# A four-block sequence kernel: the state-space block's norm by batch inside the first feed-forward, its fused input weights made there

## Reference

```python
x = x + _L0_attn_ref(_layernorm(x), ...)   # 16 heads, softmax with a page mask
x = x + _L0_ffn_ref(_layernorm(x), ...)    # top-2 of 8 experts, and a shared expert
x = x + _L1_attn_ref(_layernorm(x), ...)   # state-space block
x = x + _L1_ffn_ref(_layernorm(x), ...)    # top-2 of 8 experts, and a shared expert
# start of _L1_attn_ref, x already normed:
h = x @ fc1_w.T + fc1_b
xz = h @ in_proj_w.T
xc, z = jnp.split(xz, 2, axis=-1)
u = sum((xp[:, w:w + L, :] * conv_w[:, w] for w in range(d_conv))) + conv_b   # four taps, xp is xc padded
u = jax.nn.silu(u)
```

## Time and profile before

| | |
|---|---|
| median of 3 runs | 1397.61 us (1397.1 to 1402.02) |
| the profiled execution | 1397.69 us, of which the span of its instructions is 1395.9 us |
| PE busy | 1239.8 us, 89% of the span |
| DVE busy | 1092.1 us, 78% |
| ACT busy | 851.8 us, 61% |
| POOL busy | 575.7 us, 41% |
| mean granted TensorE clock | 0.932 of full speed |

### The profile page before, as it was taken

How to read it: one execution, slowest core, us unless ns; L and a number is a source line. 1 busy time by engine, 2 the same in 40 slices (tenths; PEclk the granted TensorE clock), 3 DMA queues, 4 the chain that set the end, 5 groups by cost and what they waited for, 6 DMA issues and landing times. The chain is left out here.

```text
span 1395.9 us, 23363 instructions
## 1 busy us (share of the span) xinstructions
PE 1239.8 (89%) x8438; PEld 646.3 (46%) x8438; DVE 1092.1 (78%) x1318; ACT 851.8 (61%) x1506; POOL 575.7 (41%) x428
## 2 busy tenths in 40 slices
PE   4936999999899989899996877999999999976998
PEld 2411333334343435344443334555655556564665
DVE  5768899999899556856554966999999999864554
ACT  2523899989799643232222778989999899512221
POOL 2320010000101237666575024888888888820000
PEclk9965999999999989999996986999999999975999
DMA  4331121321211155332450001222232232111231
GB/s 111 113 115 30 52 64 46 95 67 54 77 53 50 41 98 163 99 102 95 120 96 20 0 6 47 102 93 92 96 101 91 91 104 93 61 29 24 60 62 38
DMA packets 70509, 103.09 MB, mean 74 GB/s; under 512 B 12718, under 2 KB 42230, under 8 KB 70406
## 3 DMA queue, kind: packets, MB, share of 16 engines
q1 hardware_dynamic: 69110, 100.39, 24.6%
q10 hardware_dynamic: 1296, 1.33, 0.3%
HBM read 87.92 MB, written 13.37 MB: 73 GB/s over the span
## 5 line engine op out<-in xcount | busy, mean ns | idle before, releaser
L638 DVE TENSOR_REDUCE att_found<-PS 128x2 f32<-128x1024 f32 (+2 forms) x288 | 333.3, 1219 | 18.9 <-PE PS L747 17.2
L714 ACT ACTIVATE att_prob<-PS 128x512 f32<-128x512 f32 x576 | 313.5, 596 | 46.2 <-PE PS L769 34.4
L1928 POOL TENSOR_TENSOR ms_ch<-xnT,ms_c_rows 128x1024 f32<-128x1024 f32 x103 | 243.9, 2368 | 45.6 <-PE PS L1838 33.6
L1838 PE MATMUL PS<-ms_ch,ident_sb 128*128 128x512 f32 x512 | 241.4, 594 | 0.9 <-POOL ms_ch L1928 0.9
L1889 DVE TENSOR_TENSOR_SCAN xnT<-xnT,PS 128x1024 f32<-128x1024 f32 x103 | 231.1, 2268 | 7.4 <-PE PS L1829 7.1
L1867 ACT ACTIVATE ms_scaled<-m_dtu_turns,m_bt 128x256 f32<-128x256 f32 x448 | 191.6, 495 | 29.6 <-PE PS L1829 29.6
L788 PE MATMUL PS<-att_prob,att_v 128*32 128x256 f32 (+1 forms) x2560 | 184.9, 375 | 2.8 <-ACT fr_out L703 2.6
L1829 PEld LDWEIGHTS PS<-ident_sb,ms_scaled 128*128 128x128 f32 x1024 | 120.6, 144 | 80.1 <-DVE xnT L1889 37.4
L747 PE MATMUL PS<-kr,qr 55*128 55x128 bf16 (+4 forms) x1152 | 121.6, 292 | 31.2 <-PEq L260 16.0
L1829 PE MATMUL PS<-ident_sb,ms_scaled 128*128 128x128 f32 x1024 | 137.0, 278 | 9.7 <-ACT ms_scaled L1867 4.6
L769 PE MATMUL PS<-qr,kr 55*128 55x128 bf16 (+4 forms) x1152 | 115.9, 279 | 15.7 <-ACT att_prob L714 8.4
(11 more groups left out here) (225 smaller groups left out, 1739.4 us busy)
## 6 DMA issues: line engine op xcount, KB each, us to landing
ms_c_rows<-bc_rows_dram SPq DMA_DIRECT2D x64, 512.0 KB, 3.7
f_gate_row<-gate_rows_dram SPq DMA_DIRECT2D x64, 256.0 KB, 3.5
f_mask_row<-mask_rows_dram SPq DMA_DIRECT2D x64, 128.0 KB, 3.1
qk_parts_dram<-qkv_parts SPq DMA_DIRECT2D x48, 128.0 KB, 1.9
heads_dram<-fr_out SPq DMA_DIRECT2D x16, 256.0 KB, 2.6
f_mask_row<-mask_rows_dram SPq DMA_DIRECT2D x64, 64.0 KB, 3.2
qr<-qk_parts_dram SPq DMA_DIRECT2D x32, 96.0 KB
qr<-qk_parts_dram SPq DMA_DIRECT2D x96, 32.0 KB
```

Source lines behind the costliest of these rows:

```text
L638: dve.tensor_reduce(found[:, :, pair, first:first + (n - 1) * step + 1:step], PS[:, bank:bank + 2, :].rearrange("p r (w n) -> p r w n", w= ...
L714: act.activation(prob[:, step % PROB_RING * GH + h, :], PS[:, SCORE_BANK + unit % SCORE_RING, :], ACT.Exp, scale=float(D) ** -0.5).then_in ...
L1838: last = pe.matmul(PS[:, Y_BANK + 2 * half + q, :], g.ident[:, :], ch[:, half, q * CH:(q + 1) * CH], start=n == 0, stop=n == NS - 1)
L1928: pool.tensor_tensor(ch[:, half, :], decay_then_h(s, half), c_rows[:, s % C_RING, :], ALU.mult).then_inc(ch_ready, 1)
```

## The change

- The norm of the state-space block is taken out of its block. `Front`'s methods get batches 4 to 7 (batch 4 is batch 0 for the second time, and so on). In `first_ffn`, chunks 5, 6 and 7 norm batches 0, 1 and 2: in each, DVE does `moments_half` in slot e=1, `moments_rest` in e=2, `normalize` in e=5 and e=6; POOL does `root` in e=3; PE does `turn_x` in e=6 and e=7; ACT does `store_x` in e=7 and after it. Batch 3 is normed after the last chunk's statistics, still inside the block.
- The five weights that the first products of `mamba_in` need are loaded by SP at the start of `first_ffn`, ahead of the first gate rows, into a row buffer `shared_row`, which later serves as the scan's extra half row. PE makes the fused weight in chunk 4, slot 0 (2 large and 8 small matmul instructions), ACT copies it out in slot 2.
- The block `norm_transpose` visit 1 is gone, and with it one meeting of all engines. The other eight loads (`m`: d, x_proj, dt_proj, dt_b, a_log, fc2_b; `m.last`: two) are issued by SP at the start of `mamba_in`. DVE, ACT and PE wait for `m` only behind the convolutions; POOL waits for it where it did, ahead of its add of fc2_b to X.

```diff
     g.stat_steps, g.rstd_ready, g.normed, g.transposed, g.stored = (
...
     def turn_bank(self, b, k):
-        return (k, 2 + k, k, 1 - k)[b]
+        return (k, 2 + k, k, 1 - k)[b] if b < B else k
...
     def tiles(self, b):
-        return slice(TB * b, TB * (b + 1))
+        return slice(TB * (b % B), TB * (b % B + 1))
...
+        if b < B:
+            dve.wait_ge(self.stats_done, CPB * (b + 1))
+        else:
+            dve.wait_ge(stats_done, CPB * (b - B + 1))
         steps.done(dve.tensor_tensor(tmp[:, 0, :], me, mo, ALU.add))
...
-            last = dve.tensor_scalar(self.xn[:, k, j, :], self.g.X[:, TB * b + n, :], self.mean[:, n:n + 1], self.rstd[:, n:n + 1],
+            last = dve.tensor_scalar(self.xn[:, k, j, :], self.g.X[:, TB * (b % B) + n, :], self.mean[:, n:n + 1], self.rstd[:, n:n + 1],
...
+        if (b, k) == (4, 1):
+            pe.wait_ge(self.rows_stored, 8)
+        if b >= B:
+            pe.wait_ge(self.x_stored, CPB * (b - 1) + k + 1)
         for j in range(TPC):
...
         act.wait_ge(self.transposed, c + 1)
-        act.activation(self.g.xnT[:, CH * c:CH * (c + 1)], self.g.PS[:, self.turn_bank(b, k), :], ACT.Copy).then_inc(self.x_stored, 1)
+        act.activation(self.g.xnT[:, CH * (c % NCH):CH * (c % NCH + 1)], self.g.PS[:, self.turn_bank(b, k), :], ACT.Copy).then_inc(self.x_stored, 1)
...
         @block.sync
         def _(sp):
+            for dst, src in early.pairs:
+                sp.dma_start(dst, src).then_inc(early.loaded, 16)
             for c in range(NCH):
                 for e in range(NE):
...
+                    if c >= NORM_AT and e == 3:
+                        f.root(pool, B + c - NORM_AT)
+            f.root(pool, 2 * B - 1)
 
         @block.scalar
...
                             f.store_rows(act, b)
                             f.store_row_tables(act, b)
+                    if (c, e) == (4, 2):
+                        act.wait_ge(fused, 1)
+                        act.activation(early.in_proj.rearrange("p a b -> p (a b)"), PS[:, FUSED, :], ACT.Copy).then_inc(fused_stored, 1)
+                        act.activation(early.b_in_x, PS[:, FUSED_B, 0:2 * DI], ACT.Copy).then_inc(fused_stored, 1)
+                    if c >= NORM_AT and e >= NE - 1:
+                        f.store_x(act, B + c - NORM_AT, e - NE + 1)
             chunks(act, chunk)
+            for part in range(CPB):
+                f.store_x(act, 2 * B - 1, part)
+            act.wait_ge(f.x_stored, 2 * NCH)
 
         @block.vector
...
                         f.normalize(dve, 3, part)
+                if c >= NORM_AT:
+                    b = B + c - NORM_AT
+                    if e == 1:
+                        f.moments_half(dve, b, stats_ready)
+                    if e == 2:
+                        f.moments_rest(dve, b)
+                    if e in (5, 6):
+                        f.normalize(dve, b, e - 5)
...
             staggered(dve, chunk)
             finish(NCH - 1)
             stats(NCH - 1)
-            dve.wait_ge(stats_ready, NCH)
+            f.moments(dve, 2 * B - 1, stats_ready)
+            for part in range(CPB):
+                f.normalize(dve, 2 * B - 1, part)
...
                     for b, at, part in ((2, (0, 4), 0), (2, (0, 5), 1), (3, (3, 3), 0), (3, (3, 4), 1)):
                         if (c, e) == at:
                             f.logits(pe, b, part)
+                    if (c, e) == (4, 0):
+                        pe.wait_ge(early.loaded, early.all)
+                        pe.wait_ge(f.x_stored, NCH)
+                        pe.wait_ge(f.route_steps, 3 * ROUTE_STEPS + f.SCORES)
+                        pe.matmul(PS[:, FUSED, :], early.fc1, early.in_proj.rearrange("p a b -> p (a b)"), start=True, stop=True)
+                        for j in range(2 * DI):
+                            last = pe.matmul(PS[:, FUSED_B, j:j + 1], early.in_proj[:, j, :], early.fc1_b, start=True, stop=True)
+                        last.then_inc(fused, 1)
+                    if (c, e) == (4, 7):
+                        pe.wait_ge(fused_stored, 2)
                     for b, at in ((2, (2, 0)), (3, (4, 7))):
                         if (c, e) == at:
                             f.turn_rows(pe, b)
+                    if c >= NORM_AT and e >= NE - 2:
+                        f.turn_x(pe, B + c - NORM_AT, e - NE + 2)
                 up(NS - 1, sw1[:, 1, :], x)
                 second(NE - 1)
                 third(NS - 1, sw2[:, 1, :], x)
             staggered(pe, chunk)
             finish(NCH - 1, 1)
+            for part in range(CPB):
+                f.turn_x(pe, 2 * B - 1, part)
 
 
...
+
+def mamba_early(nc, ctx, g):
+
+    m = Loads(nc, ctx, "me_w")
+    row = g.shared_row
+    m.fc1, m.in_proj, m.fc1_b = row[:, 0:P], row[:, P:5 * P].rearrange("p (j c) -> p j c", c=P), row[:, 5 * P:5 * P + 1]
+    at = 5 * P + 1
+    m.conv_w, m.conv_b = row[:, at:at + DI * KC].rearrange("p (d t) -> p d t", t=KC), row[:, at + DI * KC:at + DI * (KC + 1)]
+    at += DI * (KC + 1)
+    m.b_in_x = row[:, at:at + 2 * DI]
+    for name in ("fc1", "in_proj", "fc1_b", "conv_w", "conv_b"):
+        m.to(dict(fc1=m.fc1, in_proj=m.in_proj, fc1_b=m.fc1_b, conv_w=m.conv_w, conv_b=m.conv_b)[name], g.w[name])
+    return m
 
 
...
     m.ctx = early
-    m.fc1, m.in_proj = m.tensor("fc1", [P, P], g.w["fc1"]), m.tensor("in_proj", [P, 2 * DI, P], g.w["in_proj"])
-    m.fc1_b = m.tensor("fc1_b", [P, 1], g.w["fc1_b"])
-    m.conv_w, m.conv_b = m.tensor("conv_w", [P, DI, KC], g.w["conv_w"]), m.tensor("conv_b", [P, DI], g.w["conv_b"])
     m.x_proj = m.tensor("x_proj", [P, DI, 2 * NS + R], g.w["x_proj"])
...
-        fc1, in_proj, x_proj, dt_proj = m.fc1, m.in_proj, m.x_proj, m.dt_proj
-        fc1_b, conv_w, conv_b, dt_b, a_log, fc2_b = m.fc1_b, m.conv_w, m.conv_b, m.dt_b, m.a_log, m.fc2_b
-        w_in_x, b_in_x = sb("w_in_x", [P, 2 * DI, P]), sb("b_in_x", [P, 2 * DI])
+        x_proj, dt_proj, dt_b, a_log, fc2_b = m.x_proj, m.dt_proj, m.dt_b, m.a_log, m.fc2_b
...
         @block.sync
         def _(sp):
+            for group in (m, m.last):
+                for dst, src in group.pairs:
+                    sp.dma_start(dst, src).then_inc(group.loaded, 16)
             for c in range(NCH):
...
@@ -1563,13 +1624,9 @@
         @block.scalar
         def _(act):
             act.preload_act_table(ACT.Silu)
-            act.wait_ge(m.loaded, m.all)
+            act.wait_ge(early.loaded, early.all)
             act.wait_ge(pad_set, 1)
             act.sem_inc(xc_ready, 1)
-            act.wait_ge(fused, 1)
-            act.activation(w_in_x[:, :, :].rearrange("p a b -> p (a b)"), PS[:, 6, :], ACT.Copy).then_inc(fused_stored, 1)
-            act.activation(b_in_x[:, :], PS[:, 7, 0:2 * DI], ACT.Copy).then_inc(fused_stored, 1)
-            act.wait_ge(fused_stored, 2)
 
             def take_x(b, k, c):
                 act.wait_ge(x_done, c + 1)
...
 
             act.preload_act_table_set("natural_log_exp_and_others")
+            act.wait_ge(m.loaded, m.all)
             act.activation(m.a[:, :, :], a_log[:, :, :], ACT.Exp).then_inc(a_steps, 1)
...
         @block.vector
         def _(dve):
             dve.sem_inc(conv_steps, 2 * CONV)
-            dve.wait_ge(m.loaded, m.all)
+            dve.wait_ge(early.loaded, early.all)
...
                                 dve.wait_ge(conv_steps, steps.base + steps.n - 1)
                                 steps.mark(dve.scalar_tensor_tensor(conv[:, k, half, :], x, w, conv[:, k, half, :], ALU.mult, ALU.add))
+            dve.wait_ge(m.loaded, m.all)
             dve.wait_ge(a_steps, 1)
...
         def _(pe):
             pe.sem_inc(u_ready, 2 * DI)
             pe.sem_inc(z_ready, 2)
-            pe.wait_ge(m.loaded, m.all)
-
-            pe.matmul(PS[:, 6, :], fc1[:, :], in_proj[:, :, :].rearrange("p a b -> p (a b)"), start=True, stop=True)
-            for j in range(2 * DI):
-                last = pe.matmul(PS[:, 7, j:j + 1], in_proj[:, j, :], fc1_b[:, :], start=True, stop=True)
-            last.then_inc(fused, 1)
-            pe.wait_ge(fused_stored, 2)
             with pe.Fori(0, B) as b:
...
                     last.then_inc(z_done, 1)
             pe.wait_ge(u_ready, DI * (2 + NCH))
             pe.wait_ge(z_ready, 2 + NCH)
+            pe.wait_ge(m.loaded, m.all)
 
...
-        four_halves, one_half = g.xnT[:, :].rearrange("p (r t) -> p r t", t=T), sb("one_half", [P, T])
+        four_halves, one_half = g.xnT[:, :].rearrange("p (r t) -> p r t", t=T), g.shared_row
         c_rows, ch = sb("c_rows", [P, C_RING, T]), sb("ch", [P, DI, T])
...
         g = make_globals(nc, ctx, w, out)
+        early = mamba_early(nc, ctx, g)
         with ExitStack() as scope:
...
-            with ExitStack() as early:
-                m = mamba_loads(nc, scope, early, g)
-                norm_transpose(nc, g, 1, [m, m.last])
-                mamba_in(nc, g, m)
+            with ExitStack() as inner:
+                m = mamba_loads(nc, scope, inner, g)
```

(3 more changed lines are left out.)

25 lines of the change are left out of this document (14 added, 11 removed).

## The result

The changed kernel takes 1422.28 us in the median of 4 runs (1417.12 to 1426.54), the kernel before 1397.36 beside it (4 runs, 1393.58 to 1402.02). The ratio is 1.0163, with a 95% interval from 1.0131 to 1.0195: 22.8 us slower by the ratio (24.9 between the two medians) where 18.9 were forecast. The forecast time was 1416.6; the measured one is 5.7 above it, within the range given. The profiled execution of the changed kernel took 1421.25 us, its span is 1419.5 (before: 1395.9).

The account below looks back on a forecast made before the run. It took PE to bound the feed-forward and DVE the convolutions. Its terms, -11.8 + 18.0 + 2.1 + 2.7 + 7.9 = +18.9 on 1397.7, gave 1416.6 us, with a range of 1403 to 1425.

Parts of the forecast that it names:

- Step 1: Between the feed-forward's last statistics and the state-space block's first product: most of the norm's time goes away, -11.8 us.
- Step 2: Chunks 5 to 7: norming batches 0 to 2 beside POOL's products makes PE wait, +18.0 us.
- The second wait of 1.9: Chunks 5 and 6: PE also waits for the second normalising part of 3.05, costing 1.9 us.
- Step 3: Chunk 4: making the fused weight on a full PE costs its full price, +2.1 us.
- Step 4: Start of the feed-forward: five loads ahead of the first gate row delay it, +2.7 us.
- Step 5: First convolution: DVE's taps wait until POOL's later add of fc2_b to X ends, +7.9 us.
- The rival in which the port is shared evenly: First convolution taps: DVE and POOL share the port, so the add costs nearer 4 us; no chance given.
- Taps not blocked: First convolution: the add doesn't hold up DVE's taps, total +11.0, 1408.7 us; chance 0.15.
- Norms cheap: Feed-forward: normalising parts take 2.1 and the start is absorbed, total +9.2, 1406.9 us; chance 0.13.
- faster: Chunks 5 to 7: DVE's tiles fit between POOL's instructions, taps not blocked, total -7.0, 1390.7 us; chance 0.08.
- End not shortened: Last statistics to first product: the remaining end takes 16 of the 21.2, total 25.5, 1423.2 us; chance 0.05.
- the case with chunk 2's full price in all three chunks: Chunks 5 to 7 cost 26.2 together, with a start of 4.5; 1426.6 us, chance 0.09.

Follow-up runs that it names:

- e10: The changed kernel run and profiled again with its code unchanged; 1418.26 us.
- e2: The changed kernel with DVE's 24 normalising instructions in chunks 5, 6 and 7 left out; 1407.86 us.
- e5: The changed kernel with the tiles of batches 0 to 2 normalised by ACT instead of DVE, POOL making the bias row; 1412.84 us.
- e9: e7 with all small steps in slot 1, POOL's power one slot earlier, fused weight made behind the last chunk; median 1391.0 us, ratio to before 0.9946.
- e6: The changed kernel with fc2_b loaded early and POOL's add to X in two earlier halves; 1415.67 us.
- e1: The changed kernel with POOL's add of fc2_b to X left out; 1403.84 us.
- e11: The kernel before with POOL's add of fc2_b to X made twice; 1405.24 us.
- e3: The kernel before with only the five early loads and the fused weight in chunk 4, norm in its own block; 1402.27 us.
- e4: The changed kernel with the five early loads issued in chunk 2, not ahead of the first gate row; 1417.37 us.
- e7: The changed kernel with tiles on ACT, the add early in two halves and six early loads in chunk 2; median 1397.44 us, ratio to before 0.9991.

## Why the prediction was right

**Step 1, the end (-11.8; measured -12.8).** The mechanism held, and all its terms but one. (The terms as written add up to 753.6, not 753.8: -12.0.) The first product did not wait for the table load's end: it starts at 775.03, while the load runs until 775.53. I had let the load release PE; that is 0.6 of the 1.0 missed.

**Step 2, the norms (+18.0; measured +18.2).** The sum held, its terms less so. Forecast were 7.6 for each of chunks 5 and 6; they cost 6.60 and 6.96. The shape of the earlier trace rows repeated (3.97 and 3.04), the wait ahead of the transposes was 3.14 for 2.6. The second wait of 1.9 didn't show in after, where the products behind the first ran at a clock of 0.57 and covered it; in e10 it came, with 1.06. Chunk 7 was mis-sized: 2.8 forecast, 4.68 measured. I had put both its parts at 2.1, on the premise that POOL has no gate products left from slot 5 on. It has one, and the first part runs beside it: 3.01, with PE waiting 2.19 for it where I had 0.8. The second took 2.08, and the small steps and transposes cost at least what they do elsewhere (2.15 in e2):

```profile
750.64 1.28 POOL L1243 TENSOR_TENSOR f_xm<-xnT,f_gate_row 128x512 f32<-128x512 f32 x1
...
750.72 3.01 DVE L1026 TENSOR_SCALAR fr_xn<-X,fr_mean,fr_rstd 128x128 f32<-128x128 f32 x4 [0.81 <-POOL fr_rstd L977]
...
754.98 2.08 DVE L1026 TENSOR_SCALAR fr_xn<-X,fr_mean,fr_rstd 128x128 f32<-128x128 f32 x4
```

That the sum was met to 0.2 is luck: chunks 5 and 6 came out 1.6 below, chunk 7 1.9 above. e2 and e5 show the division: 12.6 of the 18.2 are the tiles, the rest small steps and transposes.

**Step 3, the fused weight (+2.1; measured +1.75)**, and within 0.02 of that in all nine kernels that make it in chunk 4. The eight small matmuls have one column each, not 128 as I priced them; e9 shows them at 0.95 together.

**Step 4, the loads (+2.7; size near, carrier only in part).** Seven profiles with the loads ahead of the feed-forward have a chunk 0 of 34.22 to 36.97, mean 35.2; six without (old kernels and those with the loads in chunk 2) have 30.12 to 33.73, mean 32.3. The two sets don't overlap and differ by 2.8. Part of that is where the chunk is counted from: ACT's first step comes 1.9 to 2.9 behind PE's first product of the block in twelve of the profiles, but 5.35 behind it in e9, where it stands behind ACT's own issue of a transfer that takes 4.11. Counted from PE's first product to chunk 1 the sets are 36.14 to 38.88, mean 37.2, and 33.77 to 35.59, mean 35.0: still apart, by 2.2. The step said that the first gate row would be 2.7 later. PE's first gate product starts 7.2 behind its first product of the block with the loads and 6.3 without, in the mean, so the first row carries some 0.8 (the waits ahead of it: 3.28 to 4.15, and 1.30 to 4.10). The rest comes later in the chunk. In the first profile of after it can be seen as one wait:

```profile
520.71 1.26 POOL L1243 TENSOR_TENSOR f_xm<-xnT,f_gate_row 128x512 f32<-128x512 f32 x1 [4.56 <-DMA f_gate_row<-gate_rows_dram]
...
522.03 1.12 PE L1447 MATMUL PS<-f_xm,e_w_w 128*128 128x512 f32 x2 [2.98 <-POOL f_xm L1243]
```

The other six have no such wait of PE: its later waits for POOL in chunk 0 come to 0.9 at most, and e2 and e6 have none. What carries the rest there, and whether it is the bytes of the loads (0.33 MB, not the 0.4 that I took) or the queue, is open. A single pair of profiles would have misled: before and after alone give +5.3.

**Step 5, the add (+7.9; measured +8.5).** The main step, and it held in all its parts: loads late, add at 780.13, one DVE group of 9.38 beside it. e1 takes it away, e11 makes it in the old kernel, e3 makes a third of it, and each time DVE's instruction ends just behind POOL's. The rival in which the port is shared evenly, at 4, is out. The Trainium skill, page "SBUF — State Buffer", section "Who interferes with whom", says that the lock holds for the whole instruction; the trace agrees, 8.50 of waiting behind an instruction of 8.83. My own terms give a landing at 758.5, not the 758.1 written, and so +8.3. As measured, the miss is the start: the add began 5.1 after the first product, one with the first tap, where I had it 0.9 ahead.

**What no step had: from the last tap to the scan, +4.6.** In the four profiles with the old boundary this stage takes 50.67 to 50.70. Of the nine with the new one four take the same (e1, e4, e9, e10: 50.61 to 50.73) and five more: 52.82, 55.32, 57.31, 57.60 and 57.88; the nine average 53.7. It goes together with PE's granted clock. Stretches of the kernel before: the last 10 us of the convolutions, and 5 to 10 and 10 to 15 us behind the last tap.

```profile
799.00:809.00 10.00, 2.31 (x6) 0.76 (x4) 10.00 (x17) 7.06 (x13) 0.00 (x0) 0.75 0.00 0
...
814.00:819.00 5.00, 4.59 (x18) 1.80 (x19) 0.95 (x2) 1.51 (x4) 0.00 (x0) 0.98 0.06 13
819.00:824.00 5.00, 4.74 (x19) 1.65 (x17) 2.69 (x4) 4.91 (x7) 2.00 (x1) 1.00 0.03 7
```

The changed kernel, the last 10 us of the convolutions and 10 to 30 us behind the last tap:

```profile
817.00:827.00 10.00, 0.86 (x3) 0.03 (x1) 9.98 (x17) 7.08 (x13) 0.00 (x0) 0.68 0.00 1
```

```profile
837.00:847.00 10.00, 9.74 (x35) 4.69 (x34) 5.32 (x7) 7.36 (x11) 4.52 (x2) 0.70 0.04 8
847.00:857.00 10.00, 10.00 (x43) 4.37 (x42) 6.03 (x8) 7.07 (x10) 2.23 (x2) 0.79 0.01 3
```

The whole stage, from the last tap to the scan, of before, e10, after and e6:

```profile
809.10:859.80 50.70, 42.91 (x192) 21.48 (x192) 30.97 (x43) 37.72 (x54) 18.93 (x9) 0.84 0.02 6
```

```profile
828.88:879.50 50.62, 43.05 (x192) 21.48 (x192) 30.97 (x41) 37.64 (x53) 18.89 (x8) 0.84 0.03 6
```

```profile
826.98:882.30 55.32, 47.54 (x192) 23.36 (x192) 30.97 (x42) 37.79 (x54) 18.88 (x9) 0.78 0.02 5
```

```profile
818.52:876.40 57.88, 49.93 (x192) 23.23 (x192) 30.97 (x42) 37.87 (x53) 18.88 (x8) 0.74 0.02 5
```

The work is the same to the count, 192 matmuls; DVE, ACT and POOL are as busy in all four; only PE's busy time grows as its clock falls. All thirteen profiles follow this: 0.84 in the eight of 50.6 to 50.7, 0.79 in e7 (52.82), 0.78 in after, 0.74 in e2, e5 and e6 (57.3 to 57.9). So the longer stage goes with PE's lower clock, and the profiles show nothing else that differs. Ahead of it, in the convolutions, PE had done little: 2.31 and 0.86 of 10 us. What makes the clock fall again, or come late, in some executions and not in others of the same code, I could not show. Nor is it shown that the new boundary has a part in it: its nine profiles are 3.0 longer in the mean, but if five long stages fell among thirteen by chance, the four old ones would all be spared in one case of ten, and the kernel before alone ranges from 1392.8 to 1408.7 us in its repeated runs. The measured steps, with +2.2 for chunk 0 and without the scatter of the attention and of chunks 1 to 3, are -12.8 + 18.2 + 1.8 + 2.2 + 8.5 - 0.3 = 17.6; with these 3.0 they make 20.6, near the 22.8 of the timed runs. So the five steps held within about 1 us each, one of them by errors that cancelled, and 5.2 of the 22.8 lie in no step; that the time is in the range is in that part luck.

**The rivals.** "Taps not blocked" falls by e1 and e11. "Norms cheap" and "faster" fall by e2: the tiles alone take 12.6. "End not shortened" falls by the 8.42, and the case with chunk 2's full price in all three chunks by the 18.2 for 26.2.

**Expectations that missed.** e4 forecast more than it brought: 3.2 off chunk 0 against the first profile of after, but 0.8 against the second, so the other 2.4 were scatter. e5, e6 and e2 each came out longer than their stages say, by the stage before the scan. e1 came out shorter than forecast, by 6 to 9: its scan and rest take 533.4, those of e7 533.0, and those of the eleven others 535.8 to 537.5, a third place that scatters. In e5 chunks 5 and 6 missed their 28.9 to 29.8 by 0.2, and chunk 7 its 26 by 1.4.

## What to carry to other kernels

A stage that looks half idle is not a free place for work: price each moved instruction by the neighbour that shares its port there (here 3.97 for tiles that take 1.15 with POOL idle), and try first the engine that shares none. When a gap is closed, list the long instructions that had used it as cover, and move them with their loads: one POOL instruction of 8.8 took back two thirds of a gain of 12.8. Profile a kernel twice before small differences of a stage are explained: chunk 0 differed by 2.4 and the stage before the scan by 4.7 in the same code. And look at the event from which a stage is counted: in e9 one engine's late first step made chunk 0 look 3 us shorter.
